# Two-layer conditioned transformer on one core: float32 maxima for the first six heads, a reordered layer change, ten heads' maxima ahead in layer 1

## The reference

```python
# layer 0; layer 1 is the same with a plain MLP in place of the experts
mod = silu(c) @ w_adaln + b_adaln                    # six rows of 144 per batch
h = modulate(ln(x), sh_msa, sc_msa)
q, k, v = split(h @ w_qkv + b_qkv)                   # 16 heads of 9
attn = softmax(einsum('bhqd,bhkd->bhqk', q, k) * 9 ** -0.5)
x = x + g_msa * (merge(attn @ v) @ w_proj + b_proj)
xn = modulate(ln(x), sh_mlp, sc_mlp)
cw = softmax over the 2 best of 4 of xn @ w_gate     # 4 experts
eo = gelu(xn @ w1[e] + b1[e]) @ w2[e] + b2[e]        # hidden 576
x = x + g_mlp * sum_e cw[e] * eo[e]
```

## Time and profile before

| | |
|---|---|
| runs | 435.19, 433.06, 430.83 us; median 433.06 us |
| profiled execution | 432.17 us, its span 430.3 us |
| mean granted TensorE clock | 0.947 |
| busy: PE, DVE, ACT, POOL | 381.8, 299.5, 216.6, 82.9 us |
| share of the chain that ended last: PE, DVE, DMA, ACT | 66%, 16%, 7%, 4% |

### The profile page before, as it was taken

The page is one execution under the profiler, slowest core; times in us unless marked ns, Lnnn a source line. Parts: engine busy times, 40 slices in busy tenths (PEclk is TensorE's granted clock), DMA queues, the critical chain, the costliest instruction groups (busy, mean ns, idle before and its releaser), DMA issues.

```text
span 430.3 us, 5909 instructions
## 1 busy us (share of the span) xinstructions
PE 381.8 (89%) x1938; PEld 162.5 (38%) x1938; DVE 299.5 (70%) x838; ACT 216.6 (50%) x428; POOL 82.9 (19%) x137
## 2 busy tenths in 40 slices
PE   0995689999999897999999978889979999988896
PEld 0332122233324232585856525513232333322555
DVE  7765697989887934464496346798977888952643
ACT  1245016877776784606163211056766777585420
POOL 6897799500001000000000000001000110100000
PEclk9999557999999999999999969969998999999999
DMA  6076543469100000000000441000224100000001
GB/s 184 14 88 170 180 133 90 134 206 236 60 2 2 3 0 2 0 2 1 2 0 0 128 156 49 2 0 1 76 84 144 32 3 0 3 1 0 2 0 56
DMA packets 19657, 24.12 MB, mean 56 GB/s; under 512 B 5404, under 2 KB 15904, under 8 KB 19304
## 3 DMA queue, kind: packets, MB, share of 16 engines
q1 hardware_dynamic: 14360, 21.37, 16.4%
q0 software_dynamic: 3808, 1.73, 2.7%
q10 hardware_dynamic: 1460, 0.66, 0.5%
HBM read 19.38 MB, written 4.14 MB: 55 GB/s over the span
## 4 chain that ended last, share of the span: by engine, by line
PE 66%; DVE 16%; DMA 7%; ACT 4%; SPq 4%; issue 3%; ACTq 0%; DVEq 0%
PE bank L1138 12%; PE bank L1278 10%; DVE nmax L948 9%; PE bank L1290 9%; PE bank L1254 9%; PE bank L1238 9%; PE bank L1264 3%; DMA Qs<-qk_parts 3%; ACT prob L1088 2%; PE bank L1185 2%; PE bank L1308 2%; PE bank L1241 2%; DMA w<-in_L_cond_b_adaln_dram 2%; SPq L478 2%; DMA qk_parts<-prob 1%
## 5 line engine op out<-in xcount | busy, mean ns | idle before, releaser
L948 DVE TENSOR_REDUCE nmax<-bank 128x1 f32<-128x512 f32 x256 | 165.0, 683 | 33.9 <-PE bank L1278 33.1
L1088 ACT ACTIVATE prob<-bank 128x512 f32<-128x512 f32 x256 | 135.3, 603 | 43.3 <-PE bank L1290 42.7
L1278 PE MATMUL bank<-Ks,Qs 81*128 81x512 bf16 x256 | 104.8, 420 | 20.3 <-DMA Qs<-qk_parts 13.3
L1290 PE MATMUL bank<-Qs,Ks 83*128 83x512 bf16 x256 | 97.8, 395 | 5.8 <-ACT prob L1088 4.2
L1138 PE MATMUL bank<-prob,Va 128*32 128x512 f32 x512 | 70.7, 625 | 0.2
L586 POOL DMA_DIRECT2D Qs<-mT x24 | 13.6, 566 | 285.7 <-ACT mT L1095 240.7
L1278 PEld LDWEIGHTS bank<-Ks,Qs 81*128 81x128 bf16 x256 | 25.4, 100 | 94.6 <-DVE nmax L948 50.1
L1077 ACT ACTIVATE big<-bank 128x512 f32<-128x512 f32 (+1 forms) x46 | 27.0, 597 | 47.2 <-PE bank L1241 47.1
L1254 PE MATMUL bank<-w,big 128*128 128x144 f32 (+1 forms) x320 | 44.5, 303 | 0.4 <-DVE nmax L948 0.4
L1254 PEld LDWEIGHTS bank<-w,big 128*128 128x128 f32 (+1 forms) x320 | 37.9, 189 | 6.0 <-DVE nmax L948 1.0
L1290 PEld LDWEIGHTS bank<-Qs,Ks 83*128 83x128 bf16 x256 | 25.1, 100 | 37.1 <-ACT prob L1088 16.4
(11 more groups left out here) (159 smaller groups left out, 397.9 us busy)
## 6 DMA issues: line engine op xcount, KB each, us to landing
Ks<-qk_parts SPq DMA_DIRECT2D x36, 108.0 KB
Qs<-qk_parts SPq DMA_DIRECT2D x36, 108.0 KB
qk_parts<-prob SPq DMA_DIRECT2D x4, 384.0 KB, 3.5
mod<-modulation SPq DMA_DIRECT2D x5, 288.0 KB, 5.4
Ks<-qk_parts SPq DMA_DIRECT2D x6, 216.0 KB
Qs<-qk_parts SPq DMA_DIRECT2D x6, 216.0 KB
w<-in_L_cond_w_dram SPq DMA_DIRECT2D x3, 432.0 KB, 5.2
w<-in_L_cond_w_dram SPq DMA_DIRECT2D x4, 288.0 KB, 3.6
```

What stands on the lines that cost most here:

```text
L948: V.tensor_reduce(nmax[:, half, odd * NT + k:odd * NT + k + 1], bank[:, :], AX.X, ALU.max, negate=True).then_inc(s_free, 1)
L1088: A.activation(probs[:, k % 2, j, :], bank[:, :], ACT.Exp, scale=SCALE).then_inc(t_free, 1)
L1278: M.matmul(bank[:, :], Qs[b][0:MROW, h_, k4 * P:(k4 + 1) * P], Ks[b][0:MROW, h_, :], start=True, stop=True).then_inc(s_full, 1)
L1290: M.matmul(bank[:, :], Ks[b][0:SROWS, h0 + k4, k * P:(k + 1) * P], Qs[b][0:SROWS, h0 + k4, :], start=True, stop=True).then_inc(t_full, 1)
```

## The change

- **Float32 maxima.** For the first six heads of batch 0 in layer 0 the q and k needed for the maxima are projected once more, directly in float32, each head's nine rows at partitions 0, 32 or 64 (stage `early`, three heads each, weights in `wearly` and `wearly_stk` gathered by DVE). The scores for their maxima are float32 matmuls over nine rows (stage `emax`, three heads and one query tile) that read these copies instead of `Qs` and `Ks`. They stand right behind the projection, not behind the loads. After each `emax` of the second group there is a stage `warm`: six bf16 matmuls over 128 rows and 256 columns whose result nobody reads. Slots of heads 0 to 5 still use `Qs` and `Ks`.
- **Batch 1's projection in layer 0** moves from ahead of the first slot to the gaps behind slots (0, 0) to (0, 3). Its split goes to the list `beside`, which is now advanced three times between reductions in the first ten slots of either layer.
- **DMAs.** `mT` of the first twelve pairs is sent by ACT itself; the large loads begin at slot 7; pieces of `Qs` and `Ks` for batch 1 are named for later slots in layer 0 and for slots one earlier in layer 1.
- **Layer change.** The projection of batch 0 of layer 1 comes ahead of batch 1's `fc2` of the first expert half; the bias part of the experts' sum has a stage `ybias`; maxima of ten heads are interleaved with `fc1` and `fc2` of the second half; the first four slots of layer 1 have no maxima, and batch 1's projection starts one slot earlier.

The core of the diff:

```diff
-         ("ln", 0, 1), ("qkv", 0, 0, 0, QKV), ("ada", 1, 1), ("ada", 1, 2), ("turn", 0, 1, "a"), ("qkv", 0, 1, 0, QKV)]
-    s += [("max", 0, u) for u in range(UNIT_LEAD)]
+         ("ln", 0, 1), ("qkv", 0, 0, 0, 3), ("early", 0), ("qkv", 0, 0, 3, QKV), ("emax", 0, 0), ("early", 1),
+         ("emax", 0, 1), ("turn", 0, 1, "a"), ("emax", 0, 2), ("ada", 1, 1), ("emax", 0, 3), ("ada", 1, 2),
+         ("mturn", 0), ("emax", 1, 0), ("warm", WARM), ("emax", 1, 1), ("warm", WARM), ("emax", 1, 2), ("warm", WARM),
+         ("emax", 1, 3), ("warm", WARM), ("mturn", 1)]
...
+            after[0, 0] = [("qkv", l, 1, 0, 1)]
+            after[0, 1] = [("qkv", l, 1, 1, 2)]
+            after[0, 2] = [("qkv", l, 1, 2, 3)]
+            after[0, 3] = [("qkv", l, 1, 3, QKV)]
         else:
-            after[0, 3] = [("turn", l, 1, "a")]
-            after[1, 0] = [("qkv", l, 1, 0, 1)]
-            after[1, 1] = [("qkv", l, 1, 1, 2)]
-            after[1, 2] = [("qkv", l, 1, 2, 3)]
-            after[1, 3] = [("qkv", l, 1, 3, QKV)]
+            after[0, 2] = [("turn", l, 1, "a")]
+            after[0, 3] = [("qkv", l, 1, 0, 1)]
+            after[1, 0] = [("qkv", l, 1, 1, 2)]
+            after[1, 1] = [("qkv", l, 1, 2, 3)]
+            after[1, 2] = [("qkv", l, 1, 3, QKV)]
         for g in range(B * HG):
...
-            s += [("ln", 1, 0), ("fc1", 1, 0, 0, CHH), ("turn", 1, 0, "a"), ("fc2", 1, 0, 0, 2),
-                  ("qkv", 1, 0, 0, QKV), ("fc2", 1, 0, 2, NT), ("fc1", 1, 1, 0, 5), ("max", B, 0),
-                  ("fc1", 1, 1, 5, 7), ("max", B, 1), ("fc1", 1, 1, 7, CHH)]
+            s += [("ln", 1, 0), ("fc1", 1, 0, 0, CHH - 1), ("turn", 1, 0, "a"), ("ybias", 1), ("fc1", 1, 0, CHH - 1, CHH),
+                  ("qkv", 1, 0, 0, QKV), ("fc2", 1, 0, 0, NT), ("max", B, 0), ("fc1", 1, 1, 0, 1)]
+            for j in range(1, 5):
+                s += [("max", B, j), ("fc1", 1, 1, 2 * j - 1, 2 * j + 1)]
 
             for j in range(NT):
-                s += [("max", B, 2 + j), ("fc2", 1, 1, j, j + 1)]
+                s += [("max", B, 5 + j), ("fc2", 1, 1, j, j + 1)]
+            s += [("max", B, 9)]
...
-PIECES_AT = (((0, 1), (0, 3), (1, 1), (1, 3)), ((2, 0), (2, 1), (2, 3), (3, 1)))
+PIECES_AT = (((1, 1), (1, 3), (2, 1), (2, 3)), ((1, 3), (2, 0), (2, 2), (3, 0)))
+EARLY = 6
+EG = EARLY // 2
+LATE_FROM = 7
...
     u = stage[2] if stage[0] == "max" else NT * stage[2] + stage[3] + UNIT_LEAD if stage[0] == "slot" else None
+    if stage[0] == "slot" and stage[1] and not stage[2]:
+        return None
...
+M_ACT = 12
...
-                if stage[0] == "slot" and late:
+                if stage[0] == "slot" and NT * stage[2] + stage[3] >= LATE_FROM and late:
                     done, place, source = late.pop(0)
                     sp.dma_start(place, source).then_inc(done, 16)
-                pair = turns_pair(stage)
-                if pair is not None and 2 * pair < NH:
-
-                    n, h = 2 * pair // NH, 2 * pair % NH
-                    sp.wait_ge(t_free, T_AT[i + 1])
-                    sp.dma_start(Qs[n % B][MROW:SROWS, h:h + 2, :], mT[:, pair % 2, :]).then_inc(m_in[pair % 4], 16)
...
+            def heads_early():
+
+                a = WCOLS["qkv0"][0]
+                for src, dst in ((wqkv[0][:, :], wearly), (wstk[:, a:a + 3 * C], wearly_stk)):
+                    for w in range(2):
+                        ins = V.tensor_copy(dst[:, :, w, :].rearrange("p s (j r) -> p s j r", j=G)[:, :, 0:EG, 0:HD],
+                                            src[:, w * C:w * C + EARLY * HD]
+                                            .rearrange("p (s j d) -> p s j d", j=EG, d=HD))
+                ins.then_inc(early_ready, 1)
...
+                elif kind == "emax":
+                    _, group, k = stage
+                    for h in early_heads(group):
+                        bank = take(s_at + h - EG * group)
+                        V.tensor_reduce(nmax[:, h // 2 % 2, h % 2 * NT + k:h % 2 * NT + k + 1], bank[:, :], AX.X,
+                                        ALU.max, negate=True).then_inc(s_free, 1)
...
-                    if n == B * L - 1:
+                    if b:
...
-                            if stage[1] and u < B * NH // 2:
+                            if u < B * NH // 2:
                                 advance()
+                                advance()
+                elif kind == "slot" and not stage[2]:
+                    for _ in range(8):
+                        advance()
...
+                    if pair < M_ACT:
+                        n, h = 2 * pair // NH, 2 * pair % NH
+                        act.wait_ge(t_free, T_AT[i + 1])
+                        act.dma_start(Qs[n][MROW:SROWS, h:h + 2, :], mT[:, pair % 2, :]).then_inc(m_in[pair % 4], 16)
...
+                elif kind == "early":
+                    pe.wait_ge(early_ready, 1)
+                    pe.wait_ge(t_free, turned_at(WHERE[("qkv", 0, 0, 0, 3)]))
+                    for w in range(2):
+                        bank = fill_t(t_at + w)
+                        M.matmul(bank[:, :], wearly[:, stage[1], w, :], hT["a"][0][:, :], start=True, stop=False)
+                        M.matmul(bank[:, :], wearly_stk[:, stage[1], w, :], hS["a"][0][:, :], start=False, stop=True)\
+                            .then_inc(t_full, 1)
+                elif kind == "emax":
+                    _, group, k = stage
+                    pe.wait_ge(t_free, T_AT[WHERE[("early", group)] + 1])
+                    qk = qk_early[group]
+                    for h in early_heads(group):
+                        j = h - EG * group
+                        rows = slice(P // G * j, P // G * j + HD)
+                        M.matmul(fill_s(s_at + j)[:, :], qk[rows, 0, k * P:(k + 1) * P], qk[rows, 1, :],
+                                 start=True, stop=True).then_inc(s_full, 1)
...
+                elif kind == "warm":
+                    bank = fill_t(t_at)
+                    for _ in range(stage[1]):
+                        M.matmul(bank[:, 0:2 * P], identb[:, :], ident[:, :].bitcast(BF16), start=True, stop=True)
...
-                            if k4 == 0 and h_ == lo:
+                            if k4 == 0 and (h_ == lo or n == 0 and h_ == EARLY and lo < EARLY):
```

65 lines of the change are left out of this document (45 added, 20 removed).

## The result

The changed kernel takes 441.97 us (median of 4 runs, 439.39 to 444.47), the kernel before beside it 433.17 us (median of 4): 1.0198 times as long, 95% interval 1.0154 to 1.0241. I had forecast 426.5 and a range up to 435. The profiled execution of the changed kernel has a span of 442.7 us, 12.4 more than before. It is the slowest of the four, the one of before is a little quicker than its median, so the two traces lie 12.4 apart and the medians 8.8. In what follows a median takes in every run of a kernel, and a ratio leaves out the runs that are more than 1.5% above the kernel's fastest.

The account below looks back on a forecast made before the run. PE was taken to hold two thirds of the chain, with idle and half-speed stretches where projections pass through DRAM. Span 430.3 - 3.0 - 0.5 + 0.5 + 1.0 - 3.9 = 424.4, 426.3 with 1.87 around it, stated as 426.5; range 418 to 435.

Parts of the forecast that it names:

- group 2: Second three heads' early maxima in layer 0: 2.2 us a step, 8.9 in all, last reduction at 52.3.
- Part 1: Start of layer 0: early maxima replace the wait for loads; slot (1, 0) at 74.4, -3.0 us, ends 0 and -6.0.
- rival A: Clock falls in the float32 maxima, start gives nothing: 1.6 a step, slot (1, 0) about 81, total 433; chance 0.17.
- group 1: First three heads' early maxima in layer 0: 9.2 us of PE and some 2 us waiting for DVE, done at 43.4.
- two sums 71.4 and 75.7: Start of slot (1, 0) of layer 0 by PE alone, 71.4, and by DVE alone with waits for POOL, 75.7.
- Nine waits at 0.5: DVE's nine split operations in layer 0's first slots wait for POOL 0.5 us each, 4.5 in all.
- Side by side: An emax's three nine-row matmuls take as long as one, 0.95 us, against 2.6 one after another.
- rival B: Nine-row matmuls run one after another: 435 at full clock, 445 and more at 1.2 GHz; chance 0.10.
- Part 2: DMAs moved to ACT: -0.5 us from SP's queue, +0.5 for ACT's issues, ends 0 and +2.
- Part 3: Layer change: projection 5.1 us earlier, longer interleaving, four slots without maxima; +1.0 us, ends -2.4 and +3.
- the idle 3.3 us stays: Layer change: PE has the same 10.9 us to cover the projection's way, so its idle before the first maximum remains.
- Part 4: Unit 16 of layer 1: one more slot covers the second batch's data, wait of 2.42 and slow stretch go; -3.9 us.

Follow-up runs that it names:

- e13: Changed kernel with two 128-row float32 matmuls behind seven of the eight triples of maxima, replacing the six bf16 ones behind the last four; 439.5 us, ratio 1.0116 to before.
- e3: Changed kernel with each early float32 maximum made a full-height 128-row matmul, zeros in the other rows; 444.8 us, ratio 1.0264 to before.
- e6: Changed kernel with batch 1's layer 0 projection between the second group's maxima, in place of the small matmuls; 443.6 us, ratio 1.0236 to before.
- e5: Changed kernel with POOL's split of the remaining weights held back until slot (1, 0) of layer 0; 436.4 us, ratio 1.0094 to before.
- e9: e1 with the copies of mT issued by SP and POOL again instead of ACT; 431.9 us, ratio 0.9961 to before.
- e1: Changed kernel with the old start of layer 0 and the large loads at their old slots; 432.6 us, ratio 0.9961 to before.
- e16: Changed kernel without the small matmuls and with POOL's split held back; 435.0 us, ratio 1.0034 to before.
- e11: Kernel before, with layer 1's projection ahead of all fc2 and four fc1 chunks kept ahead of the first maximum, six heads' maxima kept; 429.3 us, ratio 0.9896.
- e10: Kernel before, with only layer 1's second-batch turn and projection one slot earlier, and its pieces earlier; 432.7 us, ratio 0.9973.
- e12: Kernel before with the edits of e10 and e11 together; 428.3 us, ratio 0.9855 to before.
- e17: e12 with two full-height float32 filler matmuls behind each of the first two slots of layer 1; 427.3 us, ratio 0.9868 to before.
- e4: Changed kernel without the small bf16 matmuls between the second group's maxima; 442.7 us, ratio 1.0199 to before.
- e14: e13 with POOL's split held back as well; 436.4 us, ratio 0.9956 to before.
- e18: e17 with fillers at layer 0's start too: ten behind the second batch's projection, two behind each of six maxima; 426.8 us, ratio 0.9858 to before.

## Why the prediction was wrong

**The step that failed is the duration of a step in group 2 of Part 1, "I take 2.2 a step", and with it rival A's chance.** It assumes the full clock. The steps took 3.4 to 4.0 us (triples start at 45.98, 49.39, 53.42 and 56.83). Last reduction of the maxima: forecast 52.3, measured 60.83; group 1 ended 2.4 late (the turn of its maxima at 45.78 instead of 43.4), group 2 another 6.1. I had written rival A with a price of 1.6 a step and 6.4 in all, which is right to half a microsecond for group 2, and had the evidence against the forecast in hand (PE full and still at 0.50). I gave it 0.17 because the small matmuls "have 128 rows". They come too late: the clock is down at 40 and the first of them is at 48. The runs e13 and e3 show that it is what PE does in the maxima: with full-height float32 matmuls between them, or made full-height themselves, the same maxima leave the clock at 1.00. Both runs add rows and fill the waits for DVE's reductions at once, so which of the two the clock fell for is not shown. The Trainium skill (TensorE: Matmul & The Clock Gate, Part 1) has sustained matmul activity as what lifts the clock; e6 disagrees, with 15 us of a full PE, float32 chunks among it, at 0.50.

**Rival A's total, about 81 for slot (1, 0), was 5 short**, for two reasons. It left out group 1 (2.4), and that DVE idles 2.19 us in slot (0, 0) to (0, 1) while the first chunk runs at half clock. From DVE's last reduction of slot (0, 0) to slot (1, 0) I had 18.5 for DVE alone; it took 20.0 (65.88 to 85.92), 1.5 more. The rest is that I rounded DVE's 82.1 down to 81: 82.1 + 2.4 + 1.5 is 86.0. The forecast itself has two slips beside the clock. Of the two sums 71.4 and 75.7 the later one has to be taken, and I took 74.4 between them, 1.3 too early. And 426.3 for the profiled execution with 0.9 to the median is 427.2, not 426.5.

**POOL was priced rightly and still misjudged.** Nine waits at 0.5 were 4.5; e5 shows 3.8 for the nine, 2.0 for the small ones, 5.3 at the marker. What the forecast didn't see is what that means: without it the start breaks even at best, so the forecast of -3.0 needed a cost it had itself just added to stay hidden.

**Side by side** was right, and rival B rightly had little (0.10): 1.13 for six records against a bound of 2.6.

**Part 2** was forecast at nothing. The changed kernel loses 1.2 between slot (1, 0) and the end of layer 0 ahead of the clock's fall, and e9 leaves it within what can be told. The cost I gave to the issues on ACT is there, but small: PE waits 0.17 for ACT's exponentials four times between 90 and 129, as in e1, and in neither of the traces with these issues on SP (before, e9), 0.7 us together where I had 0.2 in each of ten slots. The wait of 0.36 for `Qs<-mT` at slot (2, 0) is gone as forecast, but one of 0.23 stands at 112.51, and e1 has two of 1.04 and 1.11.

**Part 3**, the mechanism right, a term mis-sized. First maximum: 5.1 earlier forecast, 5.7 measured (11.3 less 5.6). Interleaving up to the slots: 40.5 forecast, 41.3 measured (255.42 to 296.68). The four slots without maxima, slot (1, 0) and the first chunk: 16.1 forecast, 19.1 measured (296.68 to 315.8). A part of the missing 3.0 is the clock at 0.50 from 300 to 310. It isn't all: twelve further traces have the same stages there (e1, e3 to e9, e13 to e16), with 3 to 7 us at 0.50, and take 17.9 to 18.7, so at least 1.8 are missing in each. Where these 1.8 go is open. Over the whole layer change these traces cost 1.5 to 4.9 against the one of before, for a forecast of 1.0. My sentence that "the idle 3.3 us stays" was right (2.96) and should have been read as advice: e11 fills exactly that gap and gains.

**Part 4** came out at -4.7 for -3.9, with its slow stretch gone. But e10 shows that this is the value in the changed kernel, where DVE has no maxima to reduce in the slots ahead; on the kernel before the same edit is worth 1.2 by the ratio and 2.1 in the traces (from the last values of layer 0 to those of layer 1), since the turn waits 2.21 for DVE. Part 4 pays where Part 3 has taken the maxima out of those slots.

**Not in the sum**: falls of the clock at 173 and 412 (1.5 and 1.6 us). The first comes and goes between traces of the same instructions: up to there e10, e11, e12 and e17 are the kernel before, and e17 and e11 have a fall there (the last value matmuls but one take 1.94 in e17 and 1.52 in e11) while the three others don't. The second I take for chance as well, which wasn't tested.

## What to carry to other kernels

Price a matmul stream at both clocks before adding small-row matmuls or thinning a stage, and if the trace shows a full PE at half clock anywhere, take the half clock as the likely case: here it cost some 5 us at the start. Fillers kept the clock up where they stood ahead of the fall; behind it neither small ones nor whole chunks of the projection brought it back soon. When work is moved out of a wait, ask what the wait was hiding: the second projection lay in the shadow of a DMA and cost nothing; behind it, it put 9.2 us on DVE, which was the bound there. And when a suspected cost is removed and little moves, see what paces the stretch behind it before the suspect is dropped: without the small matmuls the first slot came 1.4 us earlier both times, of which 0.6 were left at the first values in e4, with DVE slowed by POOL behind it, and all of it in e16, with POOL out of the way.

## What the runs showed of the hardware that I had not expected

- Nine-row float32 matmuls at three row groups run side by side: 1.13 us for three heads at full clock, 2.08 at half.
- The granted clock can fall from 1.00 to 0.50 while the profile shows PE busy 4.95 of 5 us, in a mixture of nine-row and two-column matmuls, some of which wait for a bank; with 128-row float32 matmuls of 288 columns between them it stays at 1.00 through the maxima (e13, e14; and e18 with the old start's 81-row maxima). 128-row float32 matmuls of the projection behind the fall don't raise it soon: e6 stays at 0.50 from 45 to 75.
- POOL's elementwise work stretches DVE's casts from 0.43 to as much as 1.38 us and two-input operations from 0.69 to as much as 1.64, one by one, while reductions out of PSUM keep their length; POOL's own operations beside them grow from 1.28 to 1.59.
